# A four-layer graph-attention kernel: row maxima of layer 1 taken 1024 keys at a time, scores in two PSUM banks, the shift placed by DMA

## The reference

```python
def _L1_gnn_ref(x, adj, wq, bq, wk, bk, wv, bv, wo, bo):
    q = (x @ wq.T + bq).reshape(b, n, H, HD).transpose(0, 2, 1, 3)
    ...
    scores = jnp.einsum('bhnd,bhmd->bhnm', q, k) / jnp.sqrt(jnp.float32(HD))
    scores = jnp.where(adj[None, None] == 0, -jnp.inf, scores)
    attn = jnp.nan_to_num(jax.nn.softmax(scores, axis=-1), nan=0.0)
    out = jnp.einsum('bhnm,bhmd->bhnd', attn, v)
    ...
x = _layernorm(x + _L1_gnn_ref(x, adj, ...), axis=-1)
```

## Time and profile before

| | |
|---|---|
| median of 3 runs | 3119.71 us (3115.49 to 3122.32) |
| profiled execution, own time | 3143.97 us |
| its span | 3142.2 us |
| mean granted clock of TensorE | 0.837 of full |
| PE / PEld busy | 2413.1 us (77%) / 1668.6 us (53%) |
| DVE / ACT / POOL busy | 2194.8 (70%) / 1585.7 (50%) / 1829.2 us (58%) |

### The profile page before, as it was taken

One profiled execution on the slowest core, in us unless ns is written; L12 is line 12 of the kernel. 1 busy time (PEld: TensorE's weight loads), 2 busy tenths in 40 slices (PEclk: granted clock), 3 DMA queues, 4 the chain that ended last, 5 costly groups with the idle time before them and its releaser, 6 DMA issues.

```text
span 3142.2 us, 90847 instructions
## 1 busy us (share of the span) xinstructions
PE 2413.1 (77%) x33112; PEld 1668.6 (53%) x33112; DVE 2194.8 (70%) x4654; ACT 1585.7 (50%) x2273; POOL 1829.2 (58%) x1837
## 2 busy tenths in 40 slices
PE   5588888885657888888885758888466999999990
PEld 3366666664533555555554535667343666666660
DVE  4499999997656777777774335443456988888874
ACT  2344444453652444444443533444463777777775
POOL 2388888886433555555564433344323877777782
PEclk8788888887777999999997767889676988888995
DMA  7922222232653121212113641110452111111117
GB/s 236 300 73 74 73 73 73 73 74 47 192 206 85 49 54 45 56 45 52 48 46 80 185 146 42 49 32 15 132 133 56 49 48 49 39 47 49 44 25 162
DMA packets 299864, 263.65 MB, mean 84 GB/s; under 512 B 193080, under 2 KB 257080, under 8 KB 299504
## 3 DMA queue, kind: packets, MB, share of 16 engines
q1 hardware_dynamic: 294896, 241.82, 28.4%
q0 software_dynamic: 4608, 16.78, 1.5%
HBM read 162.84 MB, written 95.36 MB: 82 GB/s over the span
## 4 chain that ended last, share of the span: by engine, by line
PE 38%; issue 22%; DVE 22%; ACT 7%; POOL 3%; DMA 2%; DVEq 1%; SPq 1%; ACTq 0%; POOLq 0%
PE ps L1113 13%; PE ps L1072 4%; DVE xn L1458 4%; DVE full L1399 4%; PE ps L1010 3%; DVE full L1389 2%; PE ps L948 2%; PE ps L1053 2%; ACT xn L728 2%; PE ps L1065 2%; DVE cv L1420 2%; PE ps L1070 2%; POOL xc L334 2%; PE ps L1024 2%; PE ps L972 2%
## 5 line engine op out<-in xcount | busy, mean ns | idle before, releaser
L334 POOL TENSOR_TENSOR xc<-part 128x512 f16<-128x512 f32 x1536 | 1579.6, 1054 | 824.2 <-ACT part L865 672.5
L1113 PE MATMUL ps<-vs,part 128*128 128x33 bf16 (+1 forms) x13824 | 854.2, 189 | 45.8 <-DVEq L1490 44.5
L1113 PEld LDWEIGHTS ps<-vs,part 128*128 128x128 bf16 x13824 | 680.0, 101 | 362.3 <-issue 206.6
L1113 PE MATMUL ps<-vs,xc 128*128 128x33 bf16 (+1 forms) x9216 | 781.0, 187 | 3.8 <-issue 3.8
L1113 PEld LDWEIGHTS ps<-vs,xc 128*128 128x128 f16 x9216 | 597.5, 99 | 0.0
L865 ACT ACTIVATE part<-ps 128x512 f32<-128x512 f32 x512 | 305.8, 597 | 434.3 <-PE ps L1057 434.1
L1399 DVE CUSTOM_DVE_ANT_0 full<-ps,mask_n 128x512 bf16<-128x512 f32 x512 | 353.0, 690 | 161.9 <-DVE top L1399 61.0
L1389 DVE CUSTOM_DVE_ANT_0 full<-ps,mask_n 128x1024 bf16<-128x1024 f32 x320 | 390.4, 1220 | 108.0 <-PE ps L1010 79.4
L847 ACT ACTIVATE part<-cv,lift 128x1024 f32<-128x1024 f32 x256 | 294.8, 1152 | 322.0 <-DVE cv L1420 297.0
L1072 PE MATMUL ps<-qs,sel 128*128 128x512 f32 x640 | 420.1, 658 | 0.0
L1053 PE MATMUL ps<-qs,ks 128*128 128x512 f32 x512 | 290.6, 570 | 120.3 <-DVE cv L1420 88.2
(11 more groups left out here) (151 smaller groups left out, 3607.5 us busy)
## 6 DMA issues: line engine op xcount, KB each, us to landing
qs<-q_d SPq DMA_DIRECT2D x224, 128.0 KB
ks<-k_d SPq DMA_DIRECT2D x224, 128.0 KB
ks<-row_d SPq DMA_DIRECT2D x40, 512.0 KB
vs<-v_d SPq DMA_DIRECT2D x96, 198.0 KB
q_d<-part SPq DMA_DIRECT2D x32, 512.0 KB
k_d<-part SPq DMA_DIRECT2D x32, 512.0 KB
ctx_d<-xn SPq DMA_DIRECT2D x96, 128.0 KB, 1.7
xc<-ctx_d SPq DMA_DIRECT2D x96, 128.0 KB, 4.6
```

The lines of the kernel that those rows point to most:

```text
L334: eng.tensor_tensor(plo[:, r, :], prob[:, r, :], phi[:, r, :], ALU.subtract).then_inc(low_done(layer, u, s)[0], 1)
L1113: mm = pe.matmul(acc, half[:, r, it * P:(it + 1) * P], vs[:, n, at:at + width], start=opens and h == 0 and v == 0, stop=h == 1 and v == 1, ...
```

## The change

In layer 1, `top_scores` makes 128 queries by all 1024 keys with two matmuls into a pair of banks, 2 and 3 or 4 and 5 in turn, and `take_max` reduces the pair in one operation: eight maxima a unit, one at each odd step, each written straight into the column of `nshift`. `find_shift`, `turn_shift` and `shift_rows` are gone from layer 1. `place_shift` waits for the eighth maximum of the unit and issues eight transfers, one for each column, as in layers 2 and 3. The row of ones in the keys becomes a row of -1. The banks of scores in layer 1 are two (0 and 1) and no longer four. There are two scrap tiles, so `take_max` waits for the maximum two before it and not for the last, in layers 2 and 3 too. `half_done` of layer 1 divides before it sums the three parts, so its first operation reads PSUM, the product has 384 numbers a partition, and the sum reads SBUF.

```diff
+MAX_NEXT = ({}, {1: 6, 3: 7}, {1: 6, 2: 7}, {1: 6, 2: 7})
+MAX_AFTER = ({}, {5: 0, 7: 1, 9: 2, 11: 3, 13: 4, 15: 5}) + ({7: 0, 9: 1, 11: 2, 13: 3, 14: 4, 15: 5},) * 2
...
-ROWMS = (0, 1, 8, 8)
+ROWMS = (0, 8, 8, 8)
...
+        junks = [full[:, k, :].bitcast(BF16)[:, 0:NODES] for k in range(2)]
...
             def place_shift(layer, g, n):
...
-                sp.wait_ge(s_shift, SHIFT_CREDIT + SHIFT0[layer] + g + 1)
-                sp.dma_start(qs[96:97, n, :].bitcast(F32).rearrange("a (t p) -> a t p", p=P),
-                             shrow[:, n % 2, :].bitcast(F32)).then_inc(s_rowm[n], 16)
+                if layer == 1:
+                    sp.wait_ge(s_nmax, max_count(g + 1))
+                else:
+                    sp.wait_ge(s_shcol, SHIFT0[layer] - SHIFT0[2] + g + 1)
+                for it in range(BLOCKS):
+                    sp.dma_start(qs[96:97, n, it * P:(it + 1) * P].bitcast(F32), nshift[:, n % 2, it:it + 1]
+                                 ).then_inc(s_rowm[n], 16)
...
-                            src, more = ps[:, r % RING, :], dict(scale=SCALE)
+                            src, more = ps[:, s % 2, :], dict(scale=SCALE)
...
                 def top_scores(n, k, U):
...
+                    at = 2 + 2 * (k % 2)
+                    pe.wait_ge(s_nmax, max_count(U) + k - 1)
+                    for c in range(2):
+                        mm = pe.matmul(ps[:, at + c, :], qs[0:96, n, k * P:(k + 1) * P],
+                                       ks[0:96, n, c * HALF:(c + 1) * HALF], start=True, stop=True)
+                    mm.then_inc(s_nsc, 1)
...
-                                pe.wait_ge(s_exp, T - RING + 1)
+                                pe.wait_ge(s_exp, T - 2 + 1)
...
+                def take_max(k, U, n):
+
+
+                    dve.wait_ge(s_nmax, max_count(U) + k - 1)
                     if layer == 1:
...
+                    dve.tensor_tensor_reduce(junks[k % 2], src, mask_n[:, k, :], 1.0, least, ALU.add, ALU.max,
+                                             accum_out=dst).then_inc(s_nmax, 1)
...
+                            link(dve.tensor_tensor(sums, acc[:, :, :, 0:width],
+                                                   scale.unsqueeze(3).to_broadcast([P, blocks, parts, width]), ALU.mult))
+                            link(dve.tensor_reduce(o, sums.rearrange("p t v d -> p t d v"), AX.X, ALU.add))
```

More of the change, by code:

```diff
@@ L1014, in top_scores @@
                 def top_scores(n, k, U):
[L1016 to L1023, removed]
-                    pe.matmul(bank, qs[0:96, n, it * P:(it + 1) * P], ks[0:96, n, cut],
-                              start=True, stop=True).then_inc(s_nsc, 1)
-                def turn_shift(n, U, taken=0):
-                    pe.wait_ge(s_shcol, U + 1)
-                    if layer == 1:
-                        pe.wait_ge(s_nmax, CREDIT + TILES * (U + 1) + taken)
-                    pe.transpose(ps[0:BLOCKS, TURN_BANK, 0:P], nshift[:, n % 2, :], ident[:, :]).then_inc(s_shT, 1)
+                    at = 2 + 2 * (k % 2)
[4 more added lines that the diff above has]
+                    mm.then_inc(s_nsc, 1)
                 def body(u, first, last):
@@ L1048, in scores @@
                         if layer < 2:
-                            bank = ps[:, s % RING, :]
+                            bank = ps[:, s % (2 if layer else RING), :]
                             if layer == 0:
@@ L1150, in heads @@
+                            if tt in MAX_AFTER[1] and one_after:
+                                if MAX_AFTER[1][tt] == 0:
+                                    unit_ready((n + 2) % UNROLL, u + (n + 2) // UNROLL)
+                                top_scores((n + 2) % UNROLL, MAX_AFTER[1][tt], U + 2)
                 if layer:
                     U = SHIFT0[layer]
-                    if layer == 1:
-                        unit_ready(0, 0)
-                        for k in range(TILES):
-                            top_scores(0, k, U)
-                        turn_shift(0, U)
-                    else:
-                        for n in range(2):
-                            unit_ready(n, 0)
-                            spread(n, U + n)
@@ L1162, in heads @@
-                    if layer == 1:
-                        unit_ready(1, 0)
-                        pe.wait_ge(s_shift, SHIFT_CREDIT + U + 1)
-                        for k in range(TILES - MAX_AT):
-                            top_scores(1, k, U + 1)
+                    for n in range(2):
+                        unit_ready(n, 0)
+                        if layer > 1:
+                            spread(n, U + n)
+                            continue
+                        for k in range(BLOCKS if n == 0 else len(MAX_AFTER[1])):
+                            top_scores(n, k, U + n)
@@ L1405, in body @@
+                    if k == BLOCKS - 1 and layer > 1:
+                        dve.wait_ge(s_nmax, max_count(U + 1))
                 def body(u, first, last):
@@ L1539, in heads @@
                     dve.wait_ge(s_stk[0], stk_at(layer, 0, 0))
[L1540 to L1546 removed]
+                    for k in range(BLOCKS):
+                        take_max(k, SHIFT0[layer], 0)
+                    if layer > 1:
+                        find_shift(0, SHIFT0[layer])
+                    for k in range(len(MAX_AFTER[layer])):
+                        take_max(k, SHIFT0[layer] + 1, 1)
                     assert state["n"] == HPRE[layer]
```

132 lines of the change are left out of this document (34 added, 98 removed).

## The result

The changed kernel takes 2967.03 us (median of 4 runs, 2962.04 to 2976.06) against 3121.02 us (4 runs, 3115.49 to 3124.52) before: the ratio is 0.9506, with a 95% interval of 0.9478 to 0.9533. It is 154 us faster, where 105 were forecast, and lies 2 us inside the lower end of the stated range (2965 to 3070 us). The profiled execution took 2962.04 us.

What follows compares the result with a forecast made beforehand. No engine was full; VectorE, idle between its own operations, was taken as layer 1's slower partner. Gains of 96 (units), 4 (ahead of layer 1) and 5 us (layers 2 and 3) gave 3039, times 0.9923 = 3015 us; range 2965 to 3070.

Steps and rivals of the forecast that it cites:

- the path through SyncE: Layer 1: half output, store, eight transfers and landing set the unit after the change, 18.1 us (16.4 to 18.9), taken as 18.3.
- TensorE's own need: Layer 1 after the change: eight steps of 0.76 and eight of 1.31 us if TensorE never waits, 16.6 us a unit.
- The landing: Layer 1, from the end of issuing the eight shift transfers to the released TensorE: 2.8 us, between 1.55 and 3.06.
- VectorE's busy time: Layer 1: falls from 16.1 to 14.5 us a unit, 15.3 with idle time behind two outputs, below TensorE's.
- The branches: Layer 1's loop: their extra time, 4.95 us each, stays after the change, so no gain is counted there.
- The count of branches: Layer 1: six branches taken off the 675.3 us of 30 units, leaving 21.5 us a unit before the change.
- Thirty units: Layer 1: each falls from 21.5 to 18.3 us, 3.2 us less, together 96 us.
- The work ahead of layer 1: Maxima ahead of its first unit lose their waits, but eight transfers come for one: 4 us gained.
- The two banks: Layer 1's scores wait for the exponential two before, not four; costed at nothing, with 0.6 us of cover.
- The bound by TensorE: Rival, layer 1: transfers land early and TensorE runs through at 16.9 us a unit; 2974 us, chance 0.2.
- the clock would fall within units: Rival, layer 1: a lower-clock stretch adds 1.7 us a unit, to 20.0; 3066 us, chance 0.2.
- SyncE's issuing: Rival, layer 1: transfers issue slower beside the loads, at 1.4 us each the unit is 24.0; 3185 us, chance 0.05.

Runs made afterwards that it cites:

- e2_order: The changed kernel with layer 1's eight shift transfers placed ahead of the last unit's output store in SyncE's queue; 2947.73 us, ratio 0.9442.
- e1_scrap: The kernel before with two scrap tiles, so a maximum waits for the one two before it; 3074.88 us against 3116.52, ratio 0.9853.
- short_pool: The changed kernel with GpSimd computing only 32 of 512 columns of its low halves from layer 1's second group of four units; 2951.55 us, ratio 0.9432.
- pad5: e2_order with five empty semaphore increments on VectorE ahead of each maximum of layer 1; 2992.82 us, ratio 0.9601.
- pad8: e2_order with eight empty semaphore increments on VectorE ahead of each maximum of layer 1; 3010.81 us, ratio 0.9659.
- e3_banks: The kernel before with two PSUM banks in place of four for layer 1's scores; 3116.05 us, ratio 0.9990.
- e4_shift8: The kernel before with layer 1's shift written by eight transfers straight from the column of maxima, without transpose and copy; 3125.80 us, ratio 1.0020.

## Why the prediction was right, and where it was not

**The mechanism held.** The pace passed to the path through SyncE, with TensorE's own need just below it; e2_order shows both. That VectorE's maxima had set the pace before is shown in part: e1_scrap, which only takes the self-wait out, gives 42 us. The forecast unit was 18.3 us and the measured one is 17.32, whose parts stand beside the forecast ones:
- from the start of a unit to the end of its output 9.87 us (forecast 9.2),
- store and signal 0.84 (0.78),
- eight issues 4.99 (5.35),
- from the last issue to TensorE 1.62 (2.8).

**The landing is the mis-sized term of the path.** I took one instance in layer 3, 3.06 us, against one of 1.55 in a quiet place, with the argument that layer 1's loads stand behind the transfers, as layer 3's do. The loads of layer 1 are issued right behind them (at 1206.85) and do them no harm: 1.62 us. The list of transfers of the kernel after has a median for all of them (KB each, us from issue to landing), first in layer 1, then between 2200 and 2860 us in layer 3:

```profile
qs<-nshift SPq DMA_DIRECT2D x248, 0.5 KB, 2.0
```

```profile
qs<-nshift SPq DMA_DIRECT2D x253, 0.5 KB, 2.0
```

With 0.6 us for the last issue, 1.62 + 0.6 = 2.2 agrees, and the instance of layer 3, 3.7, was not a typical one even there. The 2 us of the Trainium skill that the prediction puts in place of its 2.8 are stated there ("DMA: Bandwidth & Descriptors", section "Anatomy of one DMA") for a transfer issued by GpSimd. They hold setup and completion together, so the measured figure beside them is the 2.2 from the last issue on, for transfers that SyncE issues. Against the short landing stands an output that comes 0.7 us later than forecast. `half_done` is not the reason (1.59 us, forecast 1.6). VectorE's low halves, at 1.08 us for 0.78, are 0.5 of it, as short_pool shows; 0.2 stay open. The same low halves, four a unit, are also 1.2 of the 1.6 us by which VectorE's busy time, 80.79 / 87 x 17.32 = 16.1 us a unit, exceeds the forecast 14.5. TensorE's own need, forecast at 16.6, is 16.85.

**The branches were the step that failed**: "The branches stay (on VectorE's side now covered by TensorE's lead, on TensorE's not): nothing." They held 5 x 5.3 = 27 us of layer 1's 150.9. The prediction took the stand at a branch as a property of branching. In the kernel before it goes with a loading of VectorE's instructions, and in the kernel after both are gone from the loop, whose VectorE part is shorter (16 maxima a unit became 8, and the shift's operations went); with them went the stretches of TensorE at the lower clock. pad5 and pad8, which only lengthen VectorE's loop, bring the loading and a cost back. What fixes the point from which a loop is loaded again stays open, and so does whether an engine with slack would hide it: in all kernels with the packets VectorE was also the slowest engine.

**The count of branches was misread too.** The prediction takes six branches off the 675.3 us, where the trace has five. With five, 675.3 - 5 x 4.95 leaves 21.7 us a unit and not 21.5, and 30 units are 5 us more.

**The other terms.** Thirty units gave 124 us (96 forecast), that is 4.1 a unit on average and 4.3 in the steady part. The work ahead of layer 1 gave about 8 (forecast 4), ahead of layers 2 and 3 7 (5); e1_scrap, with the second scrap tile alone, gives the same 7. The two banks cost nothing in the kernel before, as e3_banks shows; after the change the weight loads of the mask's product wait for ScalarE in 195 of the steps between 1040 and 1490 us, by up to 0.9 us, but TensorE's own matmuls show no such wait. Lost again were 9 us in layer 3, in which not an instruction of the loop had changed on TensorE: its five branches, counted as what the distance of two outputs exceeds 20.2 us by, cost 23 to 24 us in the kernel before, in e1_scrap and in e3_banks, 33 in the kernel after, and 40 in e4_shift8. Together 124 + 27 + 8 + 7 - 9 = 157, where 96 + 0 + 4 + 5 = 105 were forecast: the two large misses, at the units and at the branches, are of about one size and go the same way.

**The rivals.** The bound by TensorE was closest by its number (2974), but not by its mechanism: e2_order shows that it was 0.5 us a unit away. That the clock would fall within units is refuted by 1.00. SyncE's issuing takes 0.62 us a transfer, not over 1.13.

On the rule on coalescing of the Trainium skill ("DMA: Bandwidth & Descriptors", section "Rules for kernel authors") the runs say: the eight small transfers do cost, 4.99 us of SyncE's queue for each unit, but where they are issued early enough they cost nothing (e4_shift8 in layer 1, e2_order).

## What to carry to other kernels

When one queue carries both what the next unit waits for and what nobody waits for, the order in it is a free edit: here it was worth another 19 us. A stand at a loop's branch is not a fixed price: count the packets of the instruction queues, since a shorter loop may not be loaded again. Behind such a stand look at the granted clock too, but price the two apart: branches of one kernel cost the same with and without the fall. And take a latency from the median over a stretch, not from one instance.

## What the runs showed of the hardware

VectorE's difference of two SBUF operands with 128x512 results took 0.69 us beside an idle GpSimd, 1.08 us on average and up to 1.57 beside a busy one; it is the engine's own instruction that shows as longer, not a wait in the profile. The traces show the order in it. In the kernel after, between 1040 and 1500 us, 106 of VectorE's 107 low halves start while one of GpSimd's runs, and 104 of them end 0.54 to 0.56 us after GpSimd's has ended. In the kernel before, the 24 that met none of GpSimd's and the 36 that were there first took 0.69 us, and the 20 that came second again ended 0.55 us after GpSimd's. Two instances of the kernel before, each with GpSimd's last operation ahead of it:

```profile
1304.85 1.04 POOL L334 TENSOR_TENSOR xc<-part 128x512 f16<-128x512 f32 x1 [1.57 <-ACT part L865]
1305.50 0.94 DVE L334 TENSOR_TENSOR xc<-part 128x512 f16<-128x512 f32 x1
...
1320.27 1.04 POOL L334 TENSOR_TENSOR xc<-part 128x512 f16<-128x512 f32 x1 [0.88 <-ACT part L865]
...
1322.58 0.69 DVE L334 TENSOR_TENSOR xc<-part 128x512 f16<-128x512 f32 x1 [0.20 <-PE ps L1097]
```

The Trainium skill, "SBUF — State Buffer", section "SBUF: two separate sides", says that such an operation with two SBUF inputs and a GpSimd operation that reads SBUF share a port pair as an exclusive lock, which these durations fit.

The stand of TensorE at the branches of layer 3 changed from 4.7 us to 6.7 (the kernel after) and 8.0 (e4_shift8) a branch with edits in another layer's code. The stand itself goes with instruction packets as in layer 1, but on another queue, q8, in packets of 16 KB. In the kernel before, layer 1's loop (1140 to 1610 us) has these instruction packets:

```profile
q14 instruction: 32, 0.26, 0.2%
```

and none on q8; layer 3's loop (2560 to 2990 us) has these, and none on q14:

```profile
q8 instruction: 70, 1.15, 1.1%
```

In layer 1 it is VectorE that stands at the branch, in layer 3 TensorE, so q8 is taken here to be TensorE's; no edit tested that. The number of its packets does not differ between the kernels with a short and a long stand (86 to 88 between 2450 and 2980 us in e3_banks and e4_shift8), so it does not explain the difference. Where the code lies may be the reason; no run was made on that, and it stays open.
